# ScalarE makes the decay of each scan step at the beginning of the step in front of it, not in its middle

## What is computed

```python
xn = layernorm(x);  s = attention(xn);  g = silu(experts(xn));  x = x + s * g
xn = layernorm(x)
# selective scan: 512 channels, 16 states, over the 512 tokens
    dA = exp(dt_t[..., None] * A)
    ht = dA * ht + (dt_t[..., None] * B_t[:, None, :]) * x_t[..., None]
    y_t = sum(ht * C_t[:, None, :], axis=-1)
# trees: logits -> path of 7 decisions -> silu of the nodes on the path -> output
g = silu(trees(xn));  x = x + ssm(xn) * g
```

## Time and profile before

| what | us |
|---|---|
| median of 3 runs | 2681.95 |
| lowest and highest run | 2681.63, 2683.68 |
| the profiled execution | 2662.33 |
| its span, first to last instruction | 2660.2 |
| TensorE busy | 2227.6 (84%) |
| VectorE busy | 1854.1 (70%) |
| ScalarE busy | 1771.1 (67%) |
| GpSimd busy | 1738.2 (65%) |
| mean granted clock of TensorE | 0.949 of full |

### The profile page before, as it was taken

The page is one execution under the profiler, slowest core; times in us unless marked ns, Lnnn a source line. Parts: engine busy times, 40 slices in busy tenths (PEclk is TensorE's granted clock), DMA queues, the critical chain, the costliest instruction groups (busy, mean ns, idle before and its releaser), DMA issues.

```text
span 2660.2 us, 38038 instructions
## 1 busy us (share of the span) xinstructions
PE 2227.6 (84%) x13155; PEld 1413.0 (53%) x13192; DVE 1854.1 (70%) x2832; ACT 1771.1 (67%) x3282; POOL 1738.2 (65%) x1416
## 2 busy tenths in 40 slices
PE   6776989999698889898989898889888989888761
PEld 4444667775454556455655565456445645554441
DVE  5878554543347876687668767786778666788888
ACT  3556633346278776788677867786778678766862
POOL 1000264416767888887888789887977797665565
PEclk9888999999899999999999999999999999999895
DMA  4000278864555667555765485447534754377776
GB/s 161 25 21 5 83 206 236 240 201 79 95 133 120 119 136 179 117 114 114 174 125 105 94 197 117 94 107 179 117 83 90 185 115 90 87 174 166 176 168 151
DMA packets 282032, 344.50 MB, mean 130 GB/s; under 512 B 66159, under 2 KB 211504, under 8 KB 281840
## 3 DMA queue, kind: packets, MB, share of 16 engines
q0 software_dynamic: 84080, 175.67, 35.3%
q1 hardware_dynamic: 175248, 144.83, 18.8%
q10 hardware_dynamic: 22512, 21.57, 2.4%
HBM read 198.26 MB, written 26.80 MB: 85 GB/s over the span
## 4 chain that ended last, share of the span: by engine, by line
POOL 21%; PE 19%; issue 13%; ACT 11%; DVE 8%; DMA 1%; another core or an unknown queue 0%; POOLq 0%; DVEq 0%; ACTq 0%
POOL arena L1667 8%; POOL acc_sb L1645 6%; DVE bank L1542 3%; POOL arena L1673 3%; POOL arena L1683 3%; PE bank L1784 3%; PE bank L1745 2%; PE bank L1801 2%; PE bank L1947 2%; ACT PT L1024 2%; PE bank L1789 2%; PE bank L1916 2%; ACT bank L1167 2%; PE bank L1839 2%; ACT Pr L1055 1%
## 5 line engine op out<-in xcount | busy, mean ns | idle before, releaser
L1667 POOL TENSOR_TENSOR arena<-arena 128x512 f32<-128x512 f32 x512 | 875.5, 1788 | 19.4 <-DVE arena L1533 17.5
L1645 POOL DMA_INDIRECT acc_sb<-ybuf,slot_idx x256 | 423.2, 1653 | 126.0 <-DMA ybuf<-arena 62.4
L1258 DVE TENSOR_REDUCE negmax<-bank 128x1 f32<-128x512 f32 x512 | 328.6, 683 | 212.9 <-PE bank L1784 211.9
L1167 ACT ACTIVATE bank<-arena,A_sb 128x512 f32<-128x512 f32 x512 | 354.3, 696 | 166.5 <-DVE arena L1547 138.4
L1542 DVE TENSOR_TENSOR_SCAN bank<-bank,arena 128x512 f32<-128x512 f32 x320 | 390.0, 1219 | 82.7 <-ACT bank L1167 44.2
L1673 POOL TENSOR_TENSOR arena<-arena 128x512 f32<-128x512 f32 x192 | 297.2, 1548 | 214.7 <-DVE arena L1542 214.6
L1024 ACT COPY PT<-bank 128x512 f32<-128x512 f32 x512 | 297.5, 592 | 202.1 <-PE bank L1789 193.9
L1055 ACT ACTIVATE Pr<-bank,negmax 128x512 f32<-128x512 f32 x512 | 353.5, 701 | 94.9 <-DVE negmax L1258 94.5
L1784 PE MATMUL bank<-Kp,Qp 64*128 64x512 f32 x1024 | 304.5, 659 | 88.4 <-ACT PT L1024 43.7
L1789 PEld LDWEIGHTS bank<-ident,Pr 128*128 128x128 f32 x2048 | 231.9, 146 | 274.8 <-ACT Pr L1055 214.8
L1683 POOL DMA_DIRECT2D arena<-arena x255 | 283.9, 1113 | 114.6 <-DVE arena L1547 114.3
(11 more groups left out here) (215 smaller groups left out, 3707.9 us busy)
## 6 DMA issues: line engine op xcount, KB each, us to landing
arena<-arena POOLq DMA_DIRECT2D x255, 512.0 KB, 5.3
arena<-bc_dram SPq DMA_DIRECT2D x256, 256.0 KB, 3.9
ybuf<-arena ACTq DMA_DIRECT2D x64, 256.0 KB
arena<-in_w_gate SPq DMA_DIRECT2D x64, 128.0 KB, 3.0
arena<-in_w_up SPq DMA_DIRECT2D x64, 128.0 KB, 3.7
arena<-in_w_down SPq DMA_DIRECT2D x64, 128.0 KB, 4.5
arena<-in_X SPq DMA_DIRECT2D x8, 512.0 KB, 8.2
s_sb<-in_X SPq DMA_DIRECT2D x8, 512.0 KB, 6.9
```

The costliest lines, as they stand in the source:

```text
L1167: act.activation(bank[DECAY[g % 2]][:, :], dt_sb[:, size_slot(b, cb), :], ACT.Exp, scale=A_sb[:, cb, n:n + 1]).then_inc(ssm_decay, 1)
L1258: dve.tensor_reduce(negmax[:, m % RING_STAT:m % RING_STAT + 1], bank[m % RING_S_ATT][:, :], AX.X, ALU.max, negate=True).then_inc(att_max, 1)
L1645: pool.indirect_dma_start(acc_sb[:, i, :], None, ybuf, bass.IndirectOffsetOnAxis(ap=slot_idx[:, b * TILES + i, k:k + 1], axis=0), bounds_c ...
L1667: pool.tensor_tensor(st_sb[:, g % RING_S, :], u_sb[:, size_slot(b, cb), :], B_sb[:, load % RING_BC, :], ALU.mult).then_inc(ssm_input, 1)
```

## The change

`ssm_mid` goes, and ScalarE's `decay(g + 1)` is called in `ssm_step(g)`, ahead of what `beside` and the first half of the filler give ScalarE, where it stood behind both. Its waits stay the same and move with it.

```diff
@@ -1148,9 +1148,6 @@
             def ssm_step(self, g):
                 if g == 0:
                     self.decay(0)
-
-            def ssm_mid(self, g):
-
                 self.decay(g + 1)
 
             def decay(self, g):
```

## The result

The change makes the kernel slower. Median before 2681.79 us (2678.67 to 2683.68, 4 runs), after 2706.65 us (2705.40 to 2707.12, 4 runs), ratio 1.0112 with a 95% interval of 1.009 to 1.0134. The medians are 24.9 us apart and the ratio gives 30 us, so it costs some 25 to 30 us. The forecast was +7 us: the sign was right and the size was about a quarter of what was measured.

The account below looks back on a forecast made before the run. No engine alone was the bound: four in-order queues hold each other, with VectorE the bound from 2375 us on. Terms 11 + 0 - 5 + 0 - 1 + 2 = +7 us gave 2689 us, range 2667 to 2712.

Parts of the forecast that it names:

- (a): Attention beside the scan, long stretch: ScalarE's added waiting before decays delays copies and exponents; +11 us, bounds 0 and +22.6.
- (b): Trees beside the scan, long stretch: +80 us of decay waiting replaces waits before the silus; 0, else +21 us.
- (c): Scans set free in the long stretch: VectorE waits less for decays; -5 us, bounds 0 and -51.
- rival *faster: Freed scans are what the chain runs through, at tree-attention turns and in the last stretch; -17, 2665 us; chance 0.25.
- (d): Last stretch, VectorE the bound: idle time before scans only moves by one step; 0 us, bounds -17.5 and +6.
- rival *clearly slower: Trees, above all from 2375 us on: decays waiting for VectorE hold back silus; +52, 2734 us; chance 0.06.
- (e): ScalarE's table loads: 4 fewer, 177 instead of 181; -1 us, bounds 0 and -5.1.
- (f): From 2265 to 2375 us: +10 us of waiting where neither TensorE nor VectorE is full; +2 us, bounds 0 and +10.

Follow-up runs that it names:

- attention: The changed order only in steps without a tree beside the scan, the decay in the middle elsewhere, against the kernel before: 2706.65 us, ratio 1.01.
- wait_only: Kernel before, decay still in the middle, but ScalarE waits for what releases it at the beginning of the step already: 2696.29 us, ratio 1.0117.
- control: The kernel before with one blank line more, the same program: 2680.25 against 2679.68 us, ratio 1.0001.
- trees: The decay at the beginning only in steps where trees run beside the scan, in the middle elsewhere, against the kernel before: 2689.18 us, ratio 1.0032.
- behind_side: Kernel before, but the decay stands behind the step's side work and ahead of all its filler: 2691.71 us, ratio 1.0046.
- sbuf_mid: Kernel before, decay in the middle, VectorE's scan always writing to SBUF and its multiply working in place there: 2782.94 us, ratio 1.0446.
- sbuf_begin: Changed kernel, decay at the beginning, VectorE's scan always writing to SBUF and its multiply working in place there: 2802.04 us, ratio 1.0516.

## Why the prediction was right, and where its size was wrong

**What bounds the kernel: right in its directions.** Two waits that point opposite ways, and four queues that hold each other. Both moved as said (242.2 and 36.3 us against "230 to 330" and "below 40"), there are 177 table loads, and the last decay came no earlier. TensorE's wait for PT over the first six batches grew by 9.9 us (79.1 to 89.0), near the 10 that the forecast had for PT and Pr together, but for Pr it fell by 5.6 (24.9 to 19.3), and it waits 7.0 us longer for Q's copy and inv_bc.

**(a) +11, bounds 0 and 22.6: the step that failed.** Measured +25.6 in batches 0 to 5 of "attention" (+28.6 in 0 to 4), above the upper bound. Two things were wrong in it. The size of the wait: 22.6 us was taken from the old trace with all other times held still, and ScalarE's wait before decays grew by 44.0 us (73.9 to 117.9). And the cost itself: (a) priced the decay's wait alone and put at nothing that the decay's 0.69 us of work also stands ahead of what it passes. "Wait_only" has the waits early and the work not, and beside attention it loses nothing (-1.3); the change loses 18.4 us there, "attention" 25.7. Which part of that is the 0.69 us and which the two together stays open. "I take half" had no row behind it, and the slack of 117.0 us before L1024 that was to absorb the wait was not used up: in "attention" it is 122.5 us (117.6 in control). What shrank is ScalarE's wait before the exponents, 34.3 to 20.1 us.

**(b) 0 and (c) -5, trees of the long stretch: right in sum, and not tested at the size given.** Together -3.8 in "trees" for batches 0 to 5. The wait did move from the silus to the decay: in "trees" the decays' wait grew by 24.4 us (73.9 to 98.3) and the silus' fell by 25.4 (60.7 to 35.3). But +24.4 is not the +80 that (b) saw absorbed. Of the +103 us that the prediction worked out for the long stretch (a)'s part came out twice as large and (b)'s a third. Since two equal programs differ by 2.3 us there, -5 isn't shown better than 0; a gain of tens is excluded. The rival *faster* falls with that: of the 71.7 us of scans' waits for decays 35 went, and the steps with a tree got 2.6 us shorter (3.7 in "trees"), where the unchanged program's other profile has 1.3.

**(d) 0, bounds -17.5 and +6: wrong.** Measured +11 in the last two batches (365.5 to 376.5 us), and all of it again in "trees". What the prediction looked at came true: the idle time moved from scan 466 to L1561, +0.5 us there. But it looked at one place. Over these batches VectorE's wait before L1561 grew from 0.2 to 4.4 us, that before the trees' decisions L1496 from 2.3 to 6.6, and that before L1519 from 0 to 1.8: 10.3 us of the 10.9. It resembles the mechanism of the rival *clearly slower*, at a fifth of its price, and its own sign, more than 20 us of idle TensorE before L1947, was just met (20.7 us over the whole span, 13.7 before):

```profile
PE bank L1944 <- ACT Pr L1096: 20.7, 15, 5.0
```

But that sign doesn't tell a loss from a gain: "behind_side" has 6.9 of these us in the last two batches (3.0 in control, 10.7 after) and is faster than control there. VectorE's busy time in the last 267 us is 226.49 us (84.8%, forecast 88%), with the predicted waits before L1561. "Behind_side" shows that neither the earlier decay nor the silus queued behind it cost there: it has both. What it leaves ahead of the decay is the side steps, and these are what costs.

**(e) and (f).** Four table loads fewer, and no view shows their -1 apart. (f) lies inside the numbers of (a) and (d), and nothing tells it from them.

**The sum.** Terms of the prediction: 11 + 0 - 5 + 0 - 1 + 2 = 7. Measured by stretch in the profiles against control: +15.9 in the first six batches and +10.9 in the last two, 27 together. (a) and (d) were 11 together and were measured as 25.6 and 10.9. The range (to +30) held the result because it was set wide, and not because (a)'s bounds were right; that part of the hit is luck. In batch 5 after is 6.4 us faster than control, but the profile before is 4.3 faster there too. Why this batch varies, why the parts don't add up to the whole, by what way the decay's work makes attention late, and why a set of runs is 15 us longer before the first scan stays open.

## What to carry to other kernels

In an in-order queue, an operation that is moved forward can cost what it passes in two ways, by its wait and by its work: price both (here the wait alone cost nothing beside attention), and look at both waits that a place trades (here 77 us more of one bought 35 us less of the other). A bound taken from the old trace with all other times held still is no bound in a loop of engines: the wait that was put at +22.6 us came out at +44.0. The best place differs by stretch, and a move that loses as a whole can gain where its parts were measured apart. And when a variant loses as much as the change, look where it loses before you call it the cause: "wait_only" matched the change (ratios 1.0117 and 1.0112) and lost beside the trees what the change loses beside attention.

## What the runs showed of the hardware that I had not expected

VectorE's multiply of 128x512 in float32 took 692 ns on average with one input in PSUM (control), and 1738 ns with both in SBUF ("sbuf_mid", 1676 in "sbuf_begin"), with single ones between 691 and 4447 ns, while GpSimd worked on SBUF beside it. The row of control that shows the former:

```profile
L1548 DVE TENSOR_TENSOR arena<-bank,arena 128x512 f32<-128x512 f32 x319 | 220.6, 692 | 10.9
```

The Trainium skill (SBUF — State Buffer, section Who interferes with whom) says that a VectorE instruction with two inputs in SBUF contends with a GpSimd instruction that reads SBUF, and one with at most one such input doesn't. The fastest, 691 ns, and the spread agree with that. The edit as a whole cost 119 us with the decay in the middle (2782.94 against 2663.51). The expectation for "sbuf_mid" had allowed for a longer multiply, not for this size.
